# GNN layers on one core: GpSimd waits for the landing of each group's gathers

## What is computed

```python
# layer 3 (conv): y0, y1 are node features times small matrices
w = silu(edge_attr_10 @ W_fc1 / sqrt(10)) @ W_fc2 / sqrt(100)      # 128 weights an edge
x0e, x1e = y0[src], y1[src]                                        # gather by source
messages = [w00*x0e*sh0, w11*dot(x1e, sh1)/SQ3, w01*x0e*sh1, w10*x1e*sh0]
mean = segment_sum(messages, dst) / count                          # 256 values a node

# layer 4 (attention)
w_ij = mlp(edge_attr_64) + mlp(edge_attr_32)                       # 128 an edge
q, k, v = (x @ wq)[dst], (x @ wk)[src], (x @ wv)[src]              # gather by source
alpha = (q * w_ij * k).sum(per head) / 4 * edge_weight
out = segment_sum(alpha * v, dst) / 16
```

## Time and profile before

| what | us |
|---|---|
| runs, median of 3 | 9544.22 |
| runs, lowest and highest | 9513.62 and 9572.33 |
| the profiled execution, span from first to last instruction | 9589.4 |
| conv stage, from about the first gather to its end | 2760 |
| attention stage, likewise | 3106 |

### The profile page before, as it was taken

One profiled execution on the slowest core, in us unless ns is written; L12 is line 12 of the kernel. 1 busy time (PEld: TensorE's weight loads), 2 busy tenths in 40 slices (PEclk: granted clock), 3 DMA queues, 4 the chain that ended last, 5 costly groups with the idle time before them and its releaser, 6 DMA issues. The chain is left out here.

```text
span 9589.4 us, 196015 instructions
## 1 busy us (share of the span) xinstructions
PE 7798.7 (81%) x51013; PEld 5815.8 (61%) x51014; DVE 6070.5 (63%) x12579; ACT 5243.3 (55%) x9302; POOL 3242.1 (34%) x3274
## 2 busy tenths in 40 slices
PE   5999999888699978888888777777777777777775
PEld 3656666677599966566556444445555555555554
DVE  7988998899844455555555455555555555555556
ACT  3666666788577754444444333345555555555553
POOL 0000000000000015555555556644555555454554
PEclk8999999999899988888888777788888888898897
DMA  3333333566466622222222111124555555454554
GB/s 114 138 132 137 139 136 138 190 225 223 149 183 183 183 85 58 57 57 58 56 58 57 43 43 44 44 70 144 149 147 151 152 148 148 143 159 144 149 157 124
DMA packets 627968, 1178.30 MB, mean 123 GB/s; under 512 B 215083, under 2 KB 288220, under 8 KB 608469
## 3 DMA queue, kind: packets, MB, share of 16 engines
q1 hardware_dynamic: 498618, 859.56, 28.2%
q0 software_dynamic: 129280, 317.93, 11.8%
HBM read 900.47 MB, written 276.57 MB: 123 GB/s over the span
## 5 line engine op out<-in xcount | busy, mean ns | idle before, releaser
L2250 POOL DMA_INDIRECT att_kv_rows<-kv_dram,att_stage x1616 | 1607.9, 995 | 1502.8 <-DVE att_msgs L2396 1013.5
L2005 POOL DMA_INDIRECT conv_rows<-y_dram,conv_stage x1616 | 1566.7, 969 | 1198.2 <-DVE conv_msgs L2077 678.1
L851 PE MATMUL att_mlp<-mlp_w,mlp_hid 128*128 128x128 f32 x6272 | 918.9, 296 | 397.8 <-issue 391.8
L851 PEld LDWEIGHTS att_mlp<-mlp_w,mlp_hid 128*128 128x128 f32 x6272 | 824.6, 206 | 471.7 <-issue 464.9
L1974 ACT ACTIVATE conv_hid<-conv_hid_ps 100x512 f32<-100x512 f32 x408 | 243.5, 597 | 1413.1 <-DMA y_dram<-mean_nodes_both 983.8
L695 PE MATMUL conv_part<-conv_msgs,conv_hot 128*128 128x256 f32 x3232 | 931.9, 437 | 50.1 <-issue 49.0
L2014 PE MATMUL conv_hid_ps<-conv_scalars,conv_w 10*100 10x512 f32 x816 | 529.1, 731 | 387.9 <-ACT conv_hid L1974 292.7
L695 PEld LDWEIGHTS conv_part<-conv_msgs,conv_hot 128*128 128x128 f32 x3232 | 690.5, 225 | 162.2 <-issue 64.0
L2223 ACT ACTIVATE acc<-att_q_ps 128x512 f32<-128x512 f32 x404 | 239.3, 592 | 985.9 <-DMA kv_dram<-conv_nodes_qkv 571.8
L842 PE MATMUL att_mlp<-mlp_feats,mlp_w 64*128 64x512 f32 x1568 | 558.4, 769 | 260.1 <-ACT mlp_hid L862 146.6
L235 PE MATMUL count_ps<-count_cols,count_rows 128*128 128x392 bf16 x3920 | 730.1, 331 | 8.6 <-DVE count_cols L201 8.6
(11 more groups left out here) (276 smaller groups left out, 15863.0 us busy)
## 6 DMA issues: line engine op xcount, KB each, us to landing
c_dram<-count_counts SPq DMA_DIRECT2D x392, 392.0 KB, 2.3
mean_counts<-c_dram SPq DMA_DIRECT2D x343, 448.0 KB, 3.4
w_dram<-mlp_w SPq DMA_DIRECT2D x404, 256.0 KB
att_w_rows<-w_dram SPq DMA_DIRECT2D x404, 256.0 KB
soft_counts<-c_dram SPq DMA_DIRECT2D x98, 1024.0 KB, 4.9
mlp_feats<-in_feats SPq DMA_DIRECT2D x405, 192.0 KB
soft_counts<-c_dram SPq DMA_DIRECT2D x49, 1088.0 KB, 5.0
att_lanes<-lo_dram SPq DMA_DIRECT2D x404, 128.0 KB
```

Source lines behind the costliest of these rows:

```text
L851: ins = nc.tensor.matmul(self.w_ps[:, t * D:(t + 1) * D], self.hid[:, n, t * P:(t + 1) * P], self.w1[:, n, :], start=n == 0, stop=n == 2 * ...
L2005: pool.indirect_dma_start(rows[:, s, t, :], None, y_dram, bass.IndirectOffsetOnAxis(ap=stage[:, s, t:t + 1], axis=0)).then_inc(gathered[s] ...
L2250: pool.indirect_dma_start(kv_rows[:, s, t, :], None, kv_dram, bass.IndirectOffsetOnAxis(ap=stage[:, s, t:t + 1], axis=0)).then_inc(gathere ...
```

## The change

POOL waits behind each group's four gathers until all four have landed, with the same semaphore and count that DVE and SP wait for, and only then goes on to the next group's waits and gathers. This stands in both loops. Nothing else differs.

```diff
--- before.py
+++ after.py
@@ -2006,6 +2006,8 @@
                                 rows[:, s, t, :], None, y_dram,
                                 bass.IndirectOffsetOnAxis(ap=stage[:, s, t:t + 1], axis=0)).then_inc(gathered[s], 16)
 
+                        pool.wait_ge(gathered[s], 16 * T * (i + 1))
+
             @block.tensor
             def _(pe):
                 def first(s, count):
```

## The result

The changed kernel takes 9970.61 us (9966.25 to 9977.01, 4 runs), the kernel before 9537.56 us beside it (9513.62 to 9572.33, 4 runs): a ratio of 1.0451, interval 1.0422 to 1.0479, so 433 us slower. The forecast was 9902 us, 358 us slower, with 9630 to 10,110 as its range.

What follows compares the result with a forecast made beforehand. The ring of PE, ACT and DVE bounds both loops, with POOL's slot waits as the only cover. Conv's 218 us and attention's 140 make 358 us, added to the median of 9544.22: 9902 us, range 9630 to 10,110.

Steps and rivals of the forecast that it cites:

- The bound and the cover: Both loops: PE, ACT and DVE set the pace; POOL's slot waits, 678 and 1014 us, are all the cover.
- Conv's sum: Conv group on POOL: 4.88 + 1.60 + 0.79 + 0.10 = 7.37 us against 6.83, so 218 us more.
- the 0.10 for old waits and branch: Each group on POOL: the two old waits and the loop's branch, now behind the landing, cost 0.10 us.
- the forecast's 1.60: Conv: the landing, from the last gather's end until SP and DVE go on at the first group, 1.60 us.
- the restart of 0.79: POOL, both loops: from a wait's release to the next gather's start, 0.79 us, lower end 0.30.
- Attention's sum: Attention group on POOL: 5.04 + 2.00 + 0.79 + 0.10 = 7.93 us against 7.69, so 97 us more.
- the landing of 2.00: Attention: from a group's last gather's end to its landing, 2.00 us, with 2.50 as upper end.
- rival (a): Attention's landings stay late at 2.50 us: a group takes 8.43 us, 10,104 us in all; chance 0.15.
- The 43 us for lumps: Attention: added loss because slot waits come in lumps of up to 13.8 us, when POOL can't work ahead.
- No index load becomes late: Both loops: SP is three groups ahead with index loads, so the new waits make none of them late.
- (b): Both loops: shorter landing or restart nearly hides the wait, 9544 to 9641 us; chance 0.13.
- (c): Broken gather runs relieve PE's semaphores, 431 us back, if landing and restart are under 1.95 us: 9309 us; chance 0.06.

Runs made afterwards that it cites:

- the fill of 400: Kernel before, with POOL filling an unread buffer of 400 bytes a partition behind each group and waiting for that fill alone: 8957.84 us, ratio 0.9351.
- The fills: Kernel before, with POOL waiting behind each group for its fill of an unread buffer, 1400, 400 or 16 bytes a partition: ratios 0.9915, 0.9351, 0.9516.
- the moved pause at all four groups: Kernel before, with POOL waiting for the previous group's landing behind the next group's first gather, at all four groups of a pass: 9144.95 us, ratio 0.9542.
- the fill of 16: Kernel before, with POOL filling an unread buffer of 16 bytes a partition behind each group and waiting for that fill alone: 9088.02 us, ratio 0.9516.

## Why the prediction was right, and where it was off

**The bound and the cover.** That the ring of PE, ACT and DVE set the pace, and POOL's slot waits were the only cover, held: in the kernel after POOL waits for slots 2.4 us in conv and 45.4 us in attention, and its chain of gathers and pauses makes the whole time of a group. In conv DVE waits for rows in 400 of 404 groups. In attention it does so for 33.4 us alone; there it waits for SP's loads of w_rows (465.5 us) and stores of w_dram (590.1), which stand behind the same landings in SP's stream.

**Conv's sum.** 7.37 us a group was forecast and 7.37 measured. The pause in it was forecast as 1.60 + 0.79 + 0.10 = 2.49 us and measured as 2.52 in the mean. Its split was less good: the 0.10 for old waits and branch is 0.42 at the loop's end and near nothing elsewhere. The trace's packets end 1.24 us after the last gather's end, so 1.18 us pass from there to POOL's next gather; the forecast's 1.60 had been taken where SP and DVE start again, and held a part of that. Against this split the landing was 0.36 us too long and the restart of 0.79 was 0.39 too short. That they cancel, to the hundredth, is in part luck. (The 1.20 us that the prediction estimated from the Trainium skill, page "DMA: Bandwidth & Descriptors", section "Anatomy of one DMA — SWDGE (gpsimd) path", is near the 1.24 us at which the packets end by the trace. With the restart and the 0.10 added, that estimate makes a pause of 2.09 us, 0.4 us short.)

**Attention's sum** was mis-sized: 7.93 us forecast, 8.10 measured. The group's own gathers took 4.95 us, not 5.04, and the pause was 3.15 us in the mean, against 2.00 + 0.79 + 0.10 = 2.89. The step that was short is the landing of 2.00, chosen between the bounds 1.50 and 2.50. It isn't one number: the packets end 2.16, 2.37, 1.49 and 1.46 us after the last gather of slots 0 to 3. Slots 2 and 3 are close to conv; slot 0 lies beside SP's store, and without that store its packets end at 1.48, as the other run showed. So the pause fell between the forecast and the 3.39 us of rival (a). The 43 us for lumps were not there: the pace alone makes (8.10 - 7.69) x 404 = 166 of the 169 us.

**"No index load becomes late"** held, with 7.3 us in all for att_stage; before, POOL had waited 45.6 us for conv_stage, which the prediction's two parts of its idle time in conv leave out. "PE and ACT wait only through DVE" did not: PE waits 643 and 654 us for conv_scalars and mlp_feats. No cost of that shows in the kernel after, where POOL's chain is longer still.

**The median.** The 358 us were added to the median of before. Added to the profiled span they give 9947 us beside 9975.2 measured, so of the 69 us by which the forecast was short 28 lie in the span, and most of the rest is the 47 between execution and median.

**The rivals.** (b) fell: POOL has no slot wait left in conv. (c) was named with the right condition and, as far as the runs show it, the right mechanism. Its relief is real and larger than put: 625 us by the windows of the fill of 400 (231 in conv, 394 in attention) against 431. It was looked for in the earlier trace rows alone; in attention the larger fall is not in DVE's row (mlp_w, 187.1 us to 121.6 with the fill of 400) but in PE's own, from 391.8 us ahead of L851's matmuls to 25.3, which I had not read. And its condition, landing and restart under 1.95 us, decided: pauses of 0.99 and 1.31 us make conv faster than before, those of 2.14 and 2.41 slower.

**What stays open.** The fills show that a pause between groups makes both loops faster though POOL waits for no landing in it. They don't show whether it is the issue of gathers or their packets that holds PE and DVE up: conv's packets end 1.24 us after a group's last gather, so they have ended within the pauses of 1.31 and 2.14 us too. The traces say a little more, by where the "remote" waits at conv_scaled end. In the kernel before, 108 of the 133 end while POOL is idle and the packets of all gathers issued so far have ended, which is so in 18% of conv's time. With the moved pause at all four groups only 11 of the 142 end so, but 83 end in a pause of POOL with packets of its last gather still to come. So these waits end mostly in POOL's pauses, and an ended landing is not needed for it. What in the chip passes the delay on is not shown. Nor is conv with the moved pause explained, where conv_scaled waits nearly as long as before, yet a group takes 6.56 us:

```profile
DVE conv_scaled L2079 <- remote: 615.5, 142, 8.8
```

## What to carry to other kernels

Where an engine with slack gets a wait, add up its own chain (work, landing, restart, branch) and compare it with the pace of the ring: slack covers a wait up to that pace (here 6.83 - 5.22 = 1.61 us a group in conv, against 2.15 us added) and not beyond it. When one engine issues many gathers back to back, look at the other engines' "remote" and "issue" waits during these runs: a short pause may be worth more than it costs, and its length matters: of those tried here 1.31 us behind four gathers was best, where the issuing engine had just become the bound of conv and not yet that of attention. Read these waits on PE as well as on DVE.

## What the runs showed of the hardware that was not expected

Beside runs of indirect gathers on GpSimd TensorE's issue is slow and the wake-up of those who wait for it is late, though the matmuls of L2019 and L851 read nothing that is gathered: PE stands idle ahead of L851 for 391.8 us in the kernel before, 58.8 with a pause of 0.99 us behind every fourth gather and 25.3 with 1.31. At conv_scaled it is 674.5 us before, and 69.8 with 1.31 us, where POOL's pace may take a part of the wait. At 0.99 us, the fill of 16, POOL does not set conv's pace alone, and the waits of DVE and POOL are these:

```profile
DVE conv_scaled L2076 <- remote: 357.9, 113, 9.6
...
DVE conv_scaled L2076 <- PE conv_w_ps L2023: 225.7, 86, 6.1
...
POOL conv_rows L2007 <- DVE conv_msgs L2081: 201.6, 77, 4.3
```

A loop's branch behind a wait on GpSimd costs 0.42 us in conv (2.83 against 2.41 in the kernel after, 1.72 against 1.31 with the fill of 400), and a gather that follows a wait for a landing starts 1.18 us after its last packet.
